# Attention stream of an adaLN block: head projections issued two at a time in even steps instead of one in every step

## What is computed

```
h = _layernorm(x) * (1 + ca) + sa
qkv = h @ W_pack;  q, k = rope(q), rope(k);  k, v = causal_conv2(k), causal_conv2(v)
scores = q k^T / sqrt(128), masked to (j <= i) & (i - j < 128)
x = x + ga * ((softmax(scores) @ v) @ W_o)
h = _layernorm(x) * (1 + cb) + sb
x = x + gb * moe_ffn(h)          # router top 4 of 32 experts, expert weights, shared expert
```

## Time and profile before

| | us |
|---|---|
| median of 3 runs | 854.36 |
| lowest and highest of them | 852.23, 854.43 |
| the profiled execution's own time | 851.9 |
| its span, first to last instruction | 849.9 |
| PE busy in the span | 767.5 |
| DVE busy | 538.8 |
| ACT busy | 459.7 |
| POOL busy | 479.2 |

### The profile page before, as it was taken

The page is one execution under the profiler, slowest core; times in us unless marked ns, Lnnn a source line. Parts: engine busy times, 40 slices in busy tenths (PEclk is TensorE's granted clock), DMA queues, the critical chain, the costliest instruction groups (busy, mean ns, idle before and its releaser), DMA issues.

```text
span 849.9 us, 12430 instructions
## 1 busy us (share of the span) xinstructions
PE 767.5 (90%) x3882; PEld 624.1 (73%) x3882; DVE 538.8 (63%) x1665; ACT 459.7 (54%) x1156; POOL 479.2 (56%) x395
## 2 busy tenths in 40 slices
PE   4788999999999999899999999999499978888985
PEld 2477888887888888788888788887376655566663
DVE  3398776688786978877788868895541133332342
ACT  4567877767875677797566787663511111111110
POOL 0444444453464588679578589657837534646122
PEclk9989999999999999999999999999779999998998
DMA  8906300000005010002201020411741199985641
GB/s 311 344 2 193 121 1 1 1 1 2 1 2 174 20 38 32 13 2 74 76 32 43 18 69 2 149 58 58 193 165 52 33 279 263 253 207 56 177 139 50
DMA packets 70801, 78.64 MB, mean 93 GB/s; under 512 B 7977, under 2 KB 61494, under 8 KB 70737
## 3 DMA queue, kind: packets, MB, share of 16 engines
q1 hardware_dynamic: 59856, 68.70, 25.9%
q0 software_dynamic: 9728, 8.46, 5.5%
q10 hardware_dynamic: 1152, 0.69, 0.3%
HBM read 52.27 MB, written 29.75 MB: 97 GB/s over the span
## 4 chain that ended last, share of the span: by engine, by line
PE 54%; DVE 13%; issue 9%; DMA 8%; ACT 7%; POOL 4%; SPq 4%; POOLq 0%; ACTq 0%; DVEq 0%
PE PJ L1226 17%; PE OUT L1324 9%; PE U L1313 5%; DMA expert_sum<-ye,smeta 5%; PE U L1279 5%; PE U L1302 4%; PE U L1314 2%; PE U L1278 2%; ACT U L514 2%; DMA xin<-in_dram 2%; DVE prob L905 2%; PE U L1226 2%; PE XB L1226 2%; DVE U L895 1%; PE U L1470 1%
## 5 line engine op out<-in xcount | busy, mean ns | idle before, releaser
L703 POOL TENSOR_TENSOR qsw<-qsw,sinT 128x512 f32<-128x512 f32 x96 | 124.9, 1302 | 177.9 <-ACT qsw L501 176.8
L514 ACT ACTIVATE U<-U,nmax 128x128 f32<-128x128 f32 (+1 forms) x256 | 99.0, 387 | 93.5 <-DVE nmax L895 93.4
L1324 PE MATMUL OUT<-wo,oT 128*128 128x256 f32 x512 | 131.6, 380 | 0.0
L895 DVE CUSTOM_DVE_ANT_0 U<-U,mask 128x128 f32<-128x128 f32 (+1 forms) x256 | 86.6, 378 | 61.6 <-PE U L1279 61.1
L1226 PE MATMUL PJ<-hT_hi,w_hi 128*128 128x512 f32 x256 | 112.8, 441 | 0.8 <-issue 0.8
L1226 PE MATMUL PJ<-hT_lo,w_hi 128*128 128x512 f32 x256 | 102.0, 399 | 0.0
L1226 PE MATMUL PJ<-hT_hi,w_lo 128*128 128x512 f32 x256 | 101.7, 397 | 0.0
L707 POOL TENSOR_TENSOR qr<-qr,qsw 128x512 f32<-128x512 f32 x64 | 82.3, 1286 | 29.3 <-DVE qr L883 26.1
L905 DVE TENSOR_SCALAR prob<-U,rinv 128x128 f32<-128x128 f32 (+1 forms) x256 | 95.1, 413 | 4.5
L1324 PEld LDWEIGHTS OUT<-wo,oT 128*128 128x128 f32 x512 | 87.6, 191 | 6.6
L500 ACT ACTIVATE qsw<-PJ 64x512 f32<-64x512 f32 x96 | 57.0, 593 | 57.8 <-PE PJ L1226 55.9
(11 more groups left out here) (191 smaller groups left out, 1647.7 us busy)
## 6 DMA issues: line engine op xcount, KB each, us to landing
wgu<-in_dram SPq DMA_DIRECT2D x32, 352.0 KB
wd<-in_dram SPq DMA_DIRECT2D x16, 352.0 KB
expert_sum<-eq SPq DMA_DIRECT2D x2, 2176.0 KB, 15.2
wraw<-in_dram SPq DMA_DIRECT2D x8, 512.0 KB, 12.8
slot_rows<-eq SPq DMA_DIRECT2D x1, 4096.0 KB, 16.3
bcm<-mod_rows SPq DMA_DIRECT2D x8, 512.0 KB, 7.2
xe<-slot_rows SPq DMA_DIRECT2D x16, 256.0 KB, 7.5
sums<-expert_sum SPq DMA_DIRECT2D x8, 512.0 KB, 5.4
```

Source lines behind the costliest of these rows:

```text
L514: last = act.activation(U[n % 3][:, a:z], U[n % 3][:, a:z], ACT.Exp, scale=-1.0, bias=nmax[:, n % 4, j:j + 1], accum_out=rsum[:, n % 4, j: ...
L703: pool.tensor_tensor(pair3(qsw[:, n % NQSW, :]), pair3(qsw[:, n % NQSW, :]), both(sinT[:, :]), ALU.mult).then_inc(t2_done, 1)
L895: last = dve.tensor_tensor_reduce(out=U[n % 3][:, a:z], in0=U[n % 3][:, a:z], in1=mask[:, a:z], scale=-float(HD) ** -0.5, scalar=3.4e38, o ...
L1324: last = pe.matmul(OUT[b][:, t * H:(t + 1) * H], oT[:, n % NOT, t * PN:(t + 1) * PN], wo[:, head, :], start=(head == 0 and t == 0), stop=( ...
```

## The change

In the step loop of PE the call that projected head n+4 in every step is replaced. In even steps two heads are projected in a row, n+4 and n+5; in odd steps none. Nothing else in the code is changed.

```diff
-                if n + LEAD < NU:
-                    project(n + LEAD)
+
+                if n % 2 == 0:
+                    for m in (n + LEAD, n + LEAD + 1):
+                        if m < NU:
+                            project(m)
```

## The result

| | us |
|---|---|
| before, median of 4 runs | 854.03 (852.23 to 854.43) |
| after, median of 4 runs | 884.67 (884.31 to 885.14) |
| ratio, 95% interval | 1.0361 (1.0344 to 1.0377) |
| profiled execution's span, before and after | 849.9, 883.2 |

The direction was right, the size was not: +9.9 us forecast, +30.6 measured, 7.7 above the end of the range. (One execution of all that follow, of the version with output ahead and the key as it was, took 1306.11 us at a granted clock of 0.56 and is left out of its median.) From the first scores to the last the stream grew from 549.5 us to 582.3; what comes after it took 267.8 and now 269.5. So nearly all of the loss is in the stream.

What follows compares the result with a forecast made beforehand. PE was taken to bound the stream, so only waits or the clock could change. Terms 7.6 + 2.7 + 0.6 − 1.2 − 1.0 + 1.2 = +9.9 us on 851.9 gave 861.8, or 864.3 against the median; range 854 to 877.

Steps and rivals of the forecast that it cites:

- the check of DVE's order in the odd step: Odd step: normalise done by +3.62 us, wanted by PE at +4.87; fits by 1.2, or 0.5 with k_conv ahead.
- The passages: From odd to even steps weighted_v waits for ACT's copy: 0.19 us each, 40 times, 7.6 us.
- l = 4 to 10: Stretch with ACT table changes and DVE norm hooks: 27.55 us from scores to scores, +0.2 a pair, +0.6 us.
- the 2 to 3 us of the forecast: Sign expected in the trace after: scores of l = 8 waiting 2 to 3 us.
- the second projection is covered: Even step: DVE's read-out about +2.9 us, PE wants the bank at +3.9; costs nothing unless DVE is about 1 us late.
- The first rival: Colder clock after the l = 8 stall, 4 to 5 us, or ACT's margin missed, 12 us; 869 to 878 us, chance 0.22.
- l = 28: Routing-weights hook of l = 27 makes PE wait for DVE's read-out: 3 pairs × 0.9 = 2.7 us.
- The gains: Even hooks at l = 12 to 17 hide, −1.2 us; ACT's weight splits in the first pair partly regained, −1.0 us.
- The end of the stream: Three steps in a row without projection in place of two, behind a DVE hook of 2.38 us: +1.2 us.

Runs made afterwards that it cites:

- the version with output ahead and the key as it was: Changed kernel with output(n - 3) ahead of weighted_v(n - 2) in even steps, k_conv where it was; 878.08 us, ratio 1.0310.
- the key twice: Changed kernel with k_conv's instruction issued twice with the same operands; 916.2 us, ratio 1.0761.
- the three mends together: Changed kernel with k_conv first in DVE's step, output(n - 3) ahead of weighted_v in even steps, single projections at l = 4 to 9; 851.27 us, ratio 0.9993.
- the key first: Changed kernel with k_conv moved ahead of scores(n) in DVE's step; 867.45 us, ratio 1.0191.
- output ahead as well: Changed kernel with k_conv first in DVE's step and output(n - 3) ahead of weighted_v(n - 2) in even steps; 853.77 us, ratio 1.0030.

## Why the prediction was wrong in size

**The step that failed** is the check of DVE's order in the odd step. The prediction asked whether normalise is done in time for PE's transposes, and counted the convolution there only as something that stands in front of normalise: "That fits by 1.2 us, or 0.5 with k_conv (0.74) ahead of it." It never asked when the convolution's own reader wants it. The description of the kernel names that reader: the scores at n % 4 = 0 wait for `kc_done`. The numbers were on the table. DVE starts on the scores 0.85 us into the step, scores, head and read-out take 1.58 (343.87 to 345.45), the convolution 0.74: done at 0.85 + 1.58 + 0.74 = +3.17, and PE wants it at +2.51. That is 0.66 us late. Measured: done at +3.25, scores at +3.35, so the step grew by 0.85; the listed idle time is 0.69, since it is counted from the modelled end of the transposes. The prediction even used this sum, at l = 8 alone ("k_conv of l = 7 frees the scores of l = 8 about 2.7 us late"), and did not carry it to the 28 group openings elsewhere: 28 × 0.85 = 23.8 us missing. Measured, these 28 steps are 26.9 us over PE's own work, and they are not alike: 0.41 at the six that hold one of PE's hooks (before l = 12 and 24), 0.85 at eleven ordinary ones, 1.0 to 1.6 at the eleven where hooks come on top.

**The passages.** 0.19 was right to the hundredth in the step at n % 4 = 2. At n % 4 = 0 nothing was paid, since the late key gave ACT the time; with the key mended it was 0.21. So the count of places failed with the key: the trace has 25 weighted_v pairs of 0.70 at n % 4 = 2 and none at n % 4 = 0, 25 × 0.19 = 4.8 us, where 40 × 0.19 = 7.6 had been set. Once the key is mended the count holds, with 7.4 us off the stream. The Trainium skill's rule ("TensorE: Matmul & The Clock Gate", Part 2), that a weight load is pulled ahead of running matmuls, was set against this. The 0.70 in the weighted_v pairs that themselves wait for ACT's copy shows that their load is not hidden; the 0.59 where nothing waits agrees with the rule.

**l = 4 to 10.** Forecast 27.55 us, measured 29.4 in the third pair. The walk was good up to the scores of l = 8, which come 2.72 us late; behind them it lacked two things, the clock, which was left to a rival, and DVE's read-out. The timeline of PE at l = 8, and the windows before and behind the wait (clock last but two):

```profile
361.73 0.53 PE L1278 MATMUL U<-kc,qr 128*128 128x128 f32 x2 [2.56 <-issue]
362.05 1.07 PE L1279 MATMUL U<-kc,qr 128*128 128x256 f32 x2
362.90 1.06 PE L1313 MATMUL U<-pT,vN 128*128 128x256 f32 x2
...
366.34 0.48 PE L1226 MATMUL PJ<-hT_hi,w_hi 128*128 128x512 f32 x1
...
369.21 0.38 PE L1278 MATMUL U<-kc,qr 128*128 128x128 f32 x2
```

```profile
353.00:361.00 8.00, 6.03 (x31) 4.67 (x29) 5.05 (x16) 5.95 (x15) 5.74 (x6) 1.00 0.14 49
361.00:369.00 8.00, 7.27 (x31) 6.14 (x32) 7.54 (x21) 5.19 (x18) 3.05 (x3) 0.79 0.01 2
```

The wait of 2.56 is the 2 to 3 us of the forecast. Behind it weighted_v takes 1.06, the 1.2 GHz level, and the granted clock of the window is 0.79. The step l = 8 lasts 369.21 − 361.73 = 7.48 where the like step elsewhere is 5.81, 1.67 more, in all three pairs. It is tempting to put the 1.67 down to the clock, but most of it would be there at full clock. DVE comes out of its hook late, and the second projection of the pair waits for its read-out:

```profile
363.50 1.89 DVE L954 SCALAR_TENSOR_TENSOR h<-h,std,bcm 128x256 f32<-128x256 f32 x2
365.32 0.29 DVE L895 CUSTOM_DVE_ANT_0 U<-U,mask 128x128 f32<-128x128 f32 x1
...
366.25 0.67 DVE L883 TENSOR_TENSOR qr<-PJ,cosT 128x512 f32<-128x512 f32 x1
```

L954 takes 1.89 here and 0.88 one step earlier, and that alone makes the read-out 1.0 us late. The slow matmuls only cover this wait. With the key twice, PE came through the same step of the third pair at a granted clock of 1.00, behind a wait of even 3.34 us, and the wait for the read-out is seen there:

```profile
376.26 0.46 PE L1280 MATMUL U<-kc,qr 128*128 128x128 f32 x2 [3.34 <-issue]
...
381.60 0.47 PE L1228 MATMUL PJ<-hT_hi,w_hi 128*128 128x512 f32 x1 [0.76 <-DVE qr L883]
...
383.08 0.38 PE L1280 MATMUL U<-kc,qr 128*128 128x128 f32 x2
```

That step lasts 6.82 us, and 7.48 in the second pair of the same run, where the clock fell. The changed kernel's own rows give the same as an estimate: read-out at 366.25, 0.83 until the second projection and 1.48 for it as with the key twice, is 6.83 us from 361.73. So the fall costs some 0.66 and DVE's late read-out 1.0, in three pairs 2 and 3 us. The prediction had held that the second projection is covered "as long as DVE enters the even step less than about 1 us late"; at l = 8 it enters 365.32 − 361.73 = 3.59 late. The first rival had priced the clock at l = 8 at 4 to 5 us, twice too dear; it was taken for the less likely on a wait of 1.29 that had kept the pace, and the wait foreseen was twice as long.

**l = 28.** The read-out's wait at L1226, 2.7 us in the forecast, did not come. The two groups from l = 28 on grew by 2.3 us (32.8 to 35.1), which is 2 × 1.12, two ordinary groups; the late key had moved the whole step already. With the key mended, l = 28 lasts 6.46 instead of 5.94 in the third pair, half of the 0.9, and a wait for the read-out is listed there.

**The gains.** None showed. From l = 12 to 17 it took 405.05 − 381.00 = 24.05 us. 20.8 us of work became 22.2, since six projections lie between these two scores now and five did before; the rest, 1.86 against 0.41, is the key at l = 16 (1.29, more than elsewhere, behind the hook of l = 15), twice the 0.08 behind a late key, and 0.42 at l = 14, passage and hook together, where 0.38 was lost before. The forecast took 1.2 off for them. The first 12 steps took 60.3 against 58.1 where 1.0 was taken off. The end of the stream did not cost the 1.2 that it was given: 16.6 for l = 27 to 31 of the last pair, 17.2 before.

**Together.** The profiled streams differ by 32.8 us. With 1.39 a projection taken off where they moved, 21.3 of it lies in the odd steps that end at a group's first scores (net of what the kernel before lost in them), 5.9 in l = 4 to 10 of the last three pairs (late key, read-out and clock), 3.7 in the steps n % 4 = 2, where the passages are, 1.8 in the steps n % 4 = 0 less 1.0 in n % 4 = 1, and 1.0 at both ends. One stretch at the lower clock at l = 22 of the second pair is in both kernels (from 268.3 and 279.9 us) and cancels. By the experiments, one mend after another, the ratio goes from 1.0361 to 0.9993: 1.70 points for the key, 1.61 for the passages, 0.37 for the hooks, or 14.5, 13.7 and 3.2 us. The two ways cut it differently, because a mended wait uncovers the one behind it. That the three mends together take back the whole is shown by the last run; the share of each is known to some 3 us only, and that of the clock at l = 8 is worked out from the durations above.

## What to carry over

When a step on the bound engine gets shorter, list every semaphore that this engine waits on in it and in the next, and for each the position at which the other engine signals it, also those with slack today: the slack was 0.65 us for the key (3.90 against 3.25), and the change took 1.4 out of the step. A walk made for one special place is to be made once for the ordinary place, which is the one that is multiplied. And a wait without a name ("issue") at a matmul is to be read with the producer's timeline at that moment.

## What was not expected of the hardware

PE's clock did not answer to the length of a single wait alone. Behind 2.54 to 2.56 us idle at l = 8 it fell in three cases of three (0.79 in the window above). Behind 1.84 to 1.85 us, with the key first, it fell in two of three (at 350.5 and 493.9 us, not at 208), and with output ahead as well in none of three; in two other versions, at 1.84 to 1.90 us, in one of three each. Behind 3.33 to 3.34 us, with the key twice, it fell in two of three; the third kept 1.00. And it fell where PE had not waited: twelve times in these 15 profiles, once in the kernel before (268.3 us) and once in the changed one (279.9), the fall came at l = 21 or 22, behind the router's 24 matmuls of 128x34, with no wait over 0.69 us in the 10 us ahead of it. Each of these falls lasted 3.4 us, but for one of 6.8 with the key twice. What tells these cases apart stays open.

And behind a wait the first pair lasts longer: 0.70 against 0.59 for a weighted_v pair, and for a score pair 0.46 behind the key and 0.49 behind the head's copy, against 0.38. That this is the weight load is the prediction's reading. So many short waits cost more than their idle time: 0.08 idle became 0.19.
